# Rows go through the two layers in pairs, and the last seven jobs get another mix of step kinds

## The reference, cut to what matters

```python
for i in range(2):                                   # N_LAYERS
    out = _mamba_block(out, ...)                     # 64 states for each of 512 channels
x = _layernorm(x + out)
x = _layernorm(x + _L0_xattn_ref(ctx_1024, ctx_1024, x, ...))
x = _layernorm(x + _L0_ffn_ref(x, ...))              # top 2 of 8 experts, hidden 1024

def step(h, inp):                                    # inside a Mamba block, over 256 positions
    u_t, dt_t, B_t, C_t = inp
    dA = jnp.exp(dt_t[:, :, None] * A)
    h = h * dA + (dt_t * u_t)[:, :, None] * B_t[:, None, :]
    y = jnp.einsum('bds,bs->bd', h, C_t)
```

## Time and profile before

| | us |
|---|---|
| median of 3 runs | 3252.25 (3250.26 to 3255.61) |
| the profiled execution | 3255.16 |
| its span, first to last instruction | 3253.4 |
| busy: DVE, PE, POOL, ACT | 2914.1, 2873.8, 2663.1, 2623.7 |

### The profile page before, as it was taken

The page is one execution under the profiler, slowest core; times in us unless marked ns, Lnnn a source line. Parts: engine busy times, 40 slices in busy tenths (PEclk is TensorE's granted clock), DMA queues, the critical chain, the costliest instruction groups (busy, mean ns, idle before and its releaser), DMA issues.

```text
span 3253.4 us, 59651 instructions
## 1 busy us (share of the span) xinstructions
PE 2873.8 (88%) x21906; PEld 2620.1 (81%) x21906; DVE 2914.1 (90%) x2038; ACT 2623.7 (81%) x6098; POOL 2663.1 (82%) x1317
## 2 busy tenths in 40 slices
PE   6889899998988899888988899989998989899676
PEld 4888888887888788787888788888897878888566
DVE  6999999999999999999999999999999999899410
ACT  6878888887889788887979799898989879788322
POOL 4989999888989899888989898888988888878311
PEclk8999999999999999999999999999999999999788
DMA  3254442222222222222222244424352334644086
GB/s 108 95 169 157 167 147 70 66 62 74 71 68 62 67 72 70 64 67 71 61 76 59 68 148 152 129 80 157 102 180 94 103 111 157 196 156 135 31 276 210
DMA packets 285448, 358.33 MB, mean 110 GB/s; under 512 B 100555, under 2 KB 180436, under 8 KB 284773
## 3 DMA queue, kind: packets, MB, share of 16 engines
q1 hardware_dynamic: 281202, 343.75, 33.5%
q0 software_dynamic: 3072, 8.39, 0.8%
q10 hardware_dynamic: 882, 2.38, 0.2%
HBM read 303.70 MB, written 50.73 MB: 109 GB/s over the span
## 4 chain that ended last, share of the span: by engine, by line
PE 33%; ACT 24%; POOL 14%; DVE 14%; issue 12%; DMA 2%; SPq 1%; POOLq 0%; DVEq 0%; ACTq 0%
POOL hC L1107 12%; ACT dA L1320 12%; PE psY L1665 9%; DVE h L1352 9%; PE psG L1604 7%; PE psX L1646 5%; ACT xs L1291 4%; PE psX L1636 4%; PE psG L1691 3%; DVE psX L1342 3%; PE psX L1604 2%; ACT gT L1162 1%; DMA w_up<-in_w_exp 1%; ACT scratch L1159 1%; PE psX L1628 1%
## 5 line engine op out<-in xcount | busy, mean ns | idle before, releaser
L1107 POOL TENSOR_TENSOR hC<-h,cb 128x1024 f32<-128x1024 f32 x1024 | 2404.0, 2371 | 374.7 <-DVE h L1352 336.5
L1352 DVE TENSOR_TENSOR_SCAN h<-dA,psX 128x1024 f32<-128x1024 f32 (+1 forms) x1101 | 2300.4, 2126 | 102.7 <-ACT dA L1320 35.9
L1320 ACT ACTIVATE dA<-dt,negA 128x255 f32<-128x255 f32 x4096 | 1720.0, 505 | 158.1 <-DVE h L1352 156.6
L1665 PE MATMUL psY<-ident,hC 128*128 128x128 f32 x8192 | 1088.3, 277 | 13.0 <-POOL hC L1107 10.8
L1665 PEld LDWEIGHTS psY<-ident,hC 128*128 128x128 f32 x8192 | 948.1, 143 | 25.3 <-POOL hC L1107 21.8
L1646 PE MATMUL psX<-diag_b,dtuT 128*128 128x128 f32 x4080 | 516.0, 281 | 54.9 <-DVE h L1352 52.8
L1646 PEld LDWEIGHTS psX<-diag_b,dtuT 128*128 128x128 f32 x4080 | 490.0, 195 | 87.7 <-issue 82.8
L1342 DVE TENSOR_TENSOR psX<-dtu,psX 128x1024 f32<-128x1024 f32 x411 | 496.8, 1209 | 19.5 <-PE psX L1628 18.9
L1636 PE MATMUL psX<-ident,xs 128*128 128x128 f32 x2864 | 388.4, 280 | 111.3 <-ACT xs L1291 69.5
L1291 ACT ACTIVATE xs<-dtuT,bT 128x512 f32<-128x512 f32 x716 | 476.8, 719 | 0.2
L1636 PEld LDWEIGHTS psX<-ident,xs 128*128 128x128 f32 x2864 | 326.6, 143 | 165.2 <-ACT xs L1291 91.7
(11 more groups left out here) (219 smaller groups left out, 2043.8 us busy)
## 6 DMA issues: line engine op xcount, KB each, us to landing
cb<-c_dram SPq DMA_DIRECT2D x256, 512.0 KB
w_up<-in_w_exp SPq DMA_DIRECT2D x173, 256.0 KB
w_down<-in_w_exp SPq DMA_DIRECT2D x173, 256.0 KB
diag_b<-b_dram SPq DMA_DIRECT2D x255, 128.0 KB, 3.6
x_slots<-got SPq DMA_DIRECT2D x32, 512.0 KB, 4.8
y_slots<-got SPq DMA_DIRECT2D x32, 512.0 KB, 5.0
dA<-in_w_exp SPq DMA_DIRECT2D x39, 256.0 KB, 5.0
h<-in_w_exp SPq DMA_DIRECT2D x39, 256.0 KB, 5.0
```

The costliest lines, as they stand in the source:

```text
L1107: eng.tensor_tensor(hC[i % NHC][:, :, :], h[i % NH][:, :, :], cw.to_broadcast([P, KI, L]), ALU.mult).then_inc(times_c, 1)
L1320: made = eng.activation(dA[j % NA][:, c, 1:L], dt[n % 2][:, c, 1:L], ACT.Exp, scale=negA[:, JOBS[n][0], c, s:s + 1])
L1352: made = eng.tensor_tensor_scan(h[i % NH][:, part, :].rearrange("p c t -> p (c t)"), dA[i % NA][:, part, :].rearrange("p c t -> p (c t)"), ...
L1665: made = eng.matmul(psY[:, tc, c * P:(c + 1) * P], hC[i % NHC][:, c, tc * P:(tc + 1) * P], ident[:, :], start=s == 0 and c == 0, stop=s == ...
```

## The change

`JOBS` is written in another order. Before, first and second layers alternate: (0,0), (0,1), (1,0), (0,2), (1,1), (0,3), (1,2) and so on to (0,7), (1,6), (1,7). After, both first layers of two rows are followed by both second ones: (0,0), (0,1), (1,0), (1,1), (0,2), (0,3), (1,2), (1,3) and so on. The pattern for the last jobs, `LATE`, has 26 steps `P`, 25 `T` and 13 `M` in place of 30, 25 and 9, and it holds for the last seven jobs in place of the last six. The last step stays `P`, as before.

```diff
--- before.py
+++ after.py
@@ -40,19 +40,18 @@
 ONE = DT0 + R
 
 
-JOBS = [(0, 0)]
-for _b in range(1, ROWS):
-    JOBS += [(0, _b), (1, _b - 1)]
-JOBS.append((1, ROWS - 1))
+JOBS = []
+for _b in range(0, ROWS, 2):
+    JOBS += [(0, _b), (0, _b + 1), (1, _b), (1, _b + 1)]
 NJ = len(JOBS)
 STEPS = NJ * S
 
 PLAIN, ROWS_SCALED, BY_MATRIX = "PTM"
 MATRIX_FROM = 24
 EARLY = "PMT" * 21 + "P"
-LATE = "PTPMPTPTPMTPTPT" * 4 + "PTPM"
+LATE = "PTMPT" * 12 + "PTMP"
 FIRST_JOB = "P" * 13 + "TP" * 5 + "T" + EARLY[MATRIX_FROM:]
-KINDS = FIRST_JOB + EARLY * 9 + LATE * (NJ - 10)
+KINDS = FIRST_JOB + EARLY * 8 + LATE * (NJ - 9)
 KINDS = KINDS[:-1] + PLAIN
 assert len(KINDS) == STEPS
 NDIAG = 4
```

## The result

The median is 3268.84 us (five runs, 3265.72 to 3276.70) against 3252.25 before (five runs). The ratio is 1.0053 with a 95% interval from 1.0034 to 1.0071, so the changed kernel is slower by some 16.6 us. The forecast was 3275 us in a range from 3243 to 3300. The profiled execution took 3276.70 us, 21.5 more than that of before.

A forecast was written before the change was run, and what follows sets the result against it. The loop was taken as a chain of scans narrowest at DVE, with PE next. Loop -14.0 and end +37.0 made +23.0 on the profiled 3255.16, so 3278.2, or 3275 us for the median, range 3243 to 3300.

The forecast's parts named there:

- The end: Between the sum of step 1021 and the turn, tiles on PE start row 7's attention 37.0 us later.
- A wait for a quarter: Tiles at the loop's end: PE waits 2.3 us once in the `hid` and once in the `out` pieces.
- The rival in which the weights arrive in time: End of the loop: no waits for weights, a shift of 21.1 us and 3259 us; chance 0.18.
- That of half the clock: End of the loop: PE falls to half clock between waits, a shift of 60 us and 3298 us; chance 0.15.
- the 7.7 us: A tile's length at the loop's end if a DMA cost about 2 us, in place of 11.8.
- The loop: All loop terms together: -14.0 us.
- a quarter given back: Loop: of the 25.4 us of products saved on DVE, a quarter does not arrive, +6.1 us.
- three quarters: Share of a product's time that arrives: job 10 has 9.7 us more products than job 8, is 7.4 longer.
- job 9's four products: Loop: job 9 gains 4 steps `P`, counted within the net 21 products of 1209 ns saved.
- The faster rival: Late jobs: all seven come down to 3.6 us of DVE idle time, the loop gains 47.4, 3242 us; chance 0.15.
- The layer order: Jobs 5 and 6 prepare their next job early, as job 2 does, twice 3.9: +7.8 us.
- The attention: Turn to the end: 207 us as before, tile 37 filling gaps, a clock effect of up to 4.9 us left out.

The follow-up runs named there:

- cut1025: The changed kernel without the side work of index 1025, so tiles 35 and 36 no longer stand ahead of the turn: 3248.94 us, ratio 0.9999.
- end_cut: The changed kernel with no side work placed at indices 1023 to 1025, the end of the loop: 3249.95 us, ratio 0.9985.
- small_loads: The changed kernel with weight quarters of tiles 33 to 36 loaded on 8 of 128 partitions only: 3262.38 us from a single execution.
- kinds_only: The kernel before with only the kinds of step changed, jobs alternating as before: 3299.27 us, ratio 1.0147.
- jobs_only: The kernel before with only the order of the jobs changed: 3257.50 us, ratio 1.0017.
- warm_before: The kernel before with 176 idle transposes on PE, beside the last sums and in the gaps of row 7's attention: 3242.40 us, ratio 0.9966.
- end_cut2: The changed kernel with nothing placed at the loop's end and SP not loading tile 39's rows with tile 38's: 3240.87 us, ratio 0.9957.

## Why the prediction was right

The sum forecast +23.0 us, and the medians differ by 16.6, so the median came out 6.2 us under the forecast of 3275. The two profiled executions, from which all terms are read, differ by 21.5, so the total looks better there than it is.

**The end.** The step that decided was that PE runs tiles 33 to 36 in order ahead of the sums and the turn. I had 37.0 us for it and it is 40.2. A tile was to take 11.8 us: the results of tiles 34, 35 and 36 (`yg`) follow each other after 12.3, 14.3 and 11.6 us. A wait for a quarter was to take 2.3 us and took 1.13 to 2.21. Seven such waits were to make 16.1 us and made 10.7. What I had not counted was a wait of 1.24 us for `xg` after the sums, ACT's step from `yg` to the next `xgT` (0.5 us in a tile), and the stretch at half clock. All that stands between sum and turn beside the waits for weights was to take 29.2 us and took 37.8. So two errors in opposite directions made 37.0 come that near to 40.2, and this closeness is luck, while the mechanism is not. cut1025 (24.2 us with half of the tiles) and end_cut (5.3 us with none) show the cause, and small_loads shows the part of the weights' landing. The rival in which the weights arrive in time falls with the waits above. That of half the clock came true for some 7 of the 48.5 us only. The Trainium skill ("DMA: Bandwidth & Descriptors", Anatomy of one DMA) gives its fixed cost of about 2 us for transfers that GpSimd issues, beside a further part for the bytes, which the 7.7 us leave out. The 3.01 and 5.04 us are whole landings of loads that SP issues, so they don't contradict that figure, and no run here takes the two parts asunder.

**The loop.** The sum said -14.0, and the end of the sum of step 1021 came 9.7 us earlier. From the first `hC` to the last it is 2991.8 in place of 3005.2 us. Its terms were less good than the total. Jobs 5 and 6 took the predicted 177 us, and job 4 186.2 in place of 187. Job 10 was to take 178 and took 185.6, with DVE idle for 11.0 us. So "a quarter given back" was too little for a late job without row work: the four products that were saved came back as idle time there. kinds_only agrees, whose job 10 takes 181.4 us with four products fewer, and before it was 181.1. The "three quarters" came from a comparison of job 10 with job 8, and job 10 has expert tiles too, which job 8 has not. Job 13, at 187.2 us without most of a row's work, tells the same. Up to the start of job 10 my terms make +7.8 for the order and +3.6 for job 9's four products, and job 10 starts 7.1 us later (1871.7 against 1864.6). For jobs 10 to 15 they make -25.4, and these jobs took 1158.9 us (1871.7 to 3030.6) against 1177.9 (1864.6 to 3042.5), so 19.0 less. Both parts were put down too large, with opposite signs. The faster rival, in which the late jobs lose their idle time, is false: DVE idles for 11.0, 8.6, 9.2, 7.4 and 15.5 us in jobs 10, 12, 13, 14 and 15.

**The layer order** was put at 7.8 us. jobs_only is 1.0017 of before, some 5 us (2 to 9), and its jobs 5 and 6 take 176.8 and 177.5 us, which is the step that I named. But its jobs 4 to 9 together, which hold the attention of the same three rows as before, take 1096.9 us against 1093.8. So the other jobs give part of it back, and in the profiled executions a net cost of 7.8 us is not to be seen.

**The attention.** I left the clock out, "up to 4.9 of these 10 us", and put the stretch from the turn to the end at 207 us as before. It is 198.2, and that is the step that was off. warm_before shows the clock apart, with 7.6 us. That tile 37 hides in the gaps was right. I had used the number of gaps timidly: three tiles hide there.

## What to carry to other kernels

Where a planner lets the last index of a loop take whatever still fits, look at what stands behind it on the in-order engine: here four tiles of useful work, 40 us with their waits, went ahead of the one operation that everything after waited for, and moving it behind gave more than the change itself cost. Work that is left over belongs into the gaps of the next serial chain, which took three tiles of 7.25 us for nothing (cut1025, where the clock was granted at 1.00 in the 60 us from the turn on). A saving on the engine that bounds the loop must be followed to its end, since 25 us of products less left a loop only some 10 to 15 us shorter, and it was paid with tiles that no longer fitted.

## What the runs showed of the hardware

The loop is the same sequence of instructions in the changed kernel, cut1025, end_cut, end_cut2 and small_loads up to job 15's last steps. Yet it took 2991.8, 2981.3, 2989.0, 2991.0 and 2989.4 us in the profiled executions, from the first `hC` to the last. The difference lies in single jobs, and goes with PE's granted clock. Jobs 10 and 13 of cut1025:

```profile
1867.70:2050.50 182.80, 168.80 (x1333) 155.79 (x1330) 174.34 (x93) 165.16 (x392) 161.37 (x74) 1.00 0.40 123
2430.40:2615.00 184.60, 172.97 (x1345) 158.94 (x1344) 178.01 (x106) 169.20 (x400) 164.48 (x80) 1.00 0.38 116
```

They took 182.8 and 184.6 us at a clock of 1.00. In the changed kernel the same jobs took 185.6 and 187.2 us at 0.98. A mean of 0.98 means, as an estimate, some 7 us of the job at the lower level (1.2 of 2.4 GHz), and these cost a job 2.8 and 2.6 us, although DVE and not PE is the busiest engine there. Whether the clock falls in a job differs from execution to execution. The single times of one kernel spread with it, if not strictly: of cut1025's ten, 3237.64 us had a mean clock of 0.977, the four from 3244 to 3247 had 0.974 or 0.975, and the five from 3251 to 3258.94 had 0.971 to 0.973. The clock's fall inside the attention agrees with what the Trainium skill says ("TensorE: Matmul & The Clock Gate", HAM oscillation) of products that come in bursts between waits; here 152 idle transposes in the gaps, with 24 ahead of the turn, raised it from 0.61 to 0.89.
